# A two-block transformer step: where the W1 parts are stored, and which queue loads W2

## The reference, cut to what matters

```python
def film(x, cond, w, b):
    scale, shift = jnp.split(cond @ w + b, 2, axis=-1)
    return x * (1.0 + scale[:, None, :]) + shift[:, None, :]
h = film(rmsnorm(x, norm1_w), cond, film1_w, film1_b)
Q, K, V = h @ q_w + q_b, h @ k_w + k_b, h @ v_w + v_b
attn = softmax(Q @ K^T * D ** -0.5)                  # D = 512, one head
x = x + (attn @ V) @ proj_w + proj_b
h = film(rmsnorm(x, norm2_w), cond, film2_w, film2_b)
x = x + gelu(h @ mlp_w1 + mlp_b1) @ mlp_w2 + mlp_b2  # 512 -> 2048 -> 512
```

## Time and profile before

| | |
|---|---|
| time, median of 3 runs (lowest, highest) | 1500.64 us (1499.85, 1500.69) |
| the profiled execution: its own time | 1496.73 us |
| its span in the trace | 1494.9 us |
| TensorE busy | 1472.9 us (99% of the span) |
| VectorE, ScalarE, GpSimd busy | 940.5 us (63%), 669.4 us (45%), 625.4 us (42%) |
| W1 stores | 8 of 1792 KB, median 7.4 us from issue to landing |

### The profile page before, as it was taken

One profiled execution on the slowest core, in us unless ns is written; L12 is line 12 of the kernel. 1 busy time (PEld: TensorE's weight loads), 2 busy tenths in 40 slices (PEclk: granted clock), 3 DMA queues, 4 the chain that ended last, 5 costly groups with the idle time before them and its releaser, 6 DMA issues. The chain is left out here.

```text
span 1494.9 us, 24228 instructions
## 1 busy us (share of the span) xinstructions
PE 1472.9 (99%) x8712; PEld 1196.9 (80%) x8712; DVE 940.5 (63%) x1878; ACT 669.4 (45%) x2023; POOL 625.4 (42%) x544
## 2 busy tenths in 40 slices
PE   8999999999999999998999999999999999999999
PEld 5888888888888668777888778888888888888887
DVE  6677777777776677777767653764357434764354
ACT  4656555565644455555766433432224223432210
POOL 6756667676654447665856112301114102401001
PEclk9999999999999999999999999999999999999999
DMA  7222232222215435687554765535553554545342
GB/s 256 68 90 81 79 99 72 103 76 79 78 57 165 175 120 162 235 283 257 192 183 142 269 228 185 177 136 199 201 183 117 214 190 169 176 155 200 146 133 93
DMA packets 92919, 232.57 MB, mean 156 GB/s; under 512 B 9792, under 2 KB 17984, under 8 KB 87680
## 3 DMA queue, kind: packets, MB, share of 16 engines
q1 hardware_dynamic: 92128, 230.92, 44.6%
q10 hardware_dynamic: 672, 0.10, 0.0%
HBM read 174.17 MB, written 56.82 MB: 155 GB/s over the span
## 5 line engine op out<-in xcount | busy, mean ns | idle before, releaser
L1326 ACT ACTIVATE pa<-bank,neg_max 128x128 f32<-128x128 f32 x512 | 181.2, 408 | 136.5 <-DVE neg_max L1720 136.5
L724 PE MATMUL bank<-w_hi,g_hi 128*128 128x512 f32 x512 | 200.5, 392 | 0.0
L726 PE MATMUL bank<-w_hi,g_lo 128*128 128x512 f32 x512 | 199.3, 389 | 0.0
L725 PE MATMUL bank<-w_lo,g_hi 128*128 128x512 f32 x512 | 199.3, 389 | 0.0
L1218 PE MATMUL bank<-op_hi,ring 128*128 128x512 f32 x448 | 175.0, 391 | 2.5 <-DVE u2p L2140 1.4
L1222 PE MATMUL bank<-op_hi,ring 128*128 128x512 f32 x448 | 174.3, 389 | 0.0
L1220 PE MATMUL bank<-op_lo,ring 128*128 128x512 f32 x448 | 174.3, 389 | 0.0
L2278 POOL TENSOR_TENSOR xrc<-xrc,b 128x512 f32<-128x512 f32 x32 | 50.1, 1598 | 275.2 <-DMA xrc<-x_dram 275.2
L2306 POOL TENSOR_TENSOR pa<-pa,rec 128x512 f32<-128x512 f32 x128 | 142.8, 1125 | 51.9 <-DVE rec L1743 51.8
L1573 ACT ACTIVATE sum<-sum,cols 128x512 f32<-128x512 f32 x128 | 92.0, 722 | 112.6 <-DVE sum L2140 112.6
L1326 ACT ACTIVATION_READ_ACCUMULATOR pa<-bank,neg_max 128x1 f32 x512 | 126.9, 248 | 0.0
(11 more groups left out here) (263 smaller groups left out, 3553.6 us busy)
## 6 DMA issues: line engine op xcount, KB each, us to landing
ring<-w_dram SPq DMA_DIRECT2D x32, 1792.0 KB, 7.6
rows<-st_dram SPq DMA_DIRECT2D x32, 512.0 KB, 4.7
hid_dram<-sum SPq DMA_DIRECT2D x64, 256.0 KB, 2.2
hid<-hid_dram SPq DMA_DIRECT2D x64, 256.0 KB, 2.7
w_dram<-w_parts SPq DMA_DIRECT2D x8, 1792.0 KB, 7.4
xa<-xt_in SPq DMA_DIRECT2D x32, 256.0 KB, 4.2
xra<-xt_in SPq DMA_DIRECT2D x32, 256.0 KB, 2.8
x_dram<-h SPq DMA_DIRECT2D x32, 256.0 KB, 2.0
```

Source lines behind the costliest of these rows:

```text
L724: nc.tensor.matmul(dst, w_hi, a_hi, start=start, stop=False)
L725: nc.tensor.matmul(dst, w_hi, a_lo, start=False, stop=False)
L726: return nc.tensor.matmul(dst, w_lo, a_hi, start=False, stop=stop)
L1326: last = nc.scalar.activation(pa[:, j, m, :], scores_bank[j][:, m * P:(m + 1) * P], ACT.Exp, bias=neg_max[:, j * C + m:j * C + m + 1], acc ...
```

## The change

Its parts, in the order of the diff:

- `w2_pieces`: the pieces of W2 are split at one per half round: round 1 has 1 and 2, round 2 has 3 and 4, and so on.
- `t_first` has four slots in place of two. GpSimd makes the four samples' `t_first` (`rest_first`) one after the other, ahead of the last residual's bias; VectorE's low halves `low_first` move behind the softmax of sample 3.
- SyncE stores a group's first W1 piece where both stood (behind the third residual store). The second piece is stored one group later, behind the reload of residual 3. ScalarE splits the second piece behind the squares of samples 2 and 3, no longer ahead of them. VectorE's place for it stays.
- VectorE's `mean_square` of samples 0 and 1 moves from the start of the next group to the end of this one.
- The first round of stage C runs its products in the order 4, 0, 1, 2, 3, 5, 6, with bank 4 for products 4 and 6; `copy_ptb` of the last sample moves ahead accordingly.
- W2's pieces 2 to 7 are loaded from ScalarE's queue, each behind the split of the piece before; each piece is one transfer of 512 KB. Pieces 0 and 1 stay in SyncE's queue.

```diff
-    return ((), (0,)) if p == 0 else ((1,), ()) if p == 1 else ((2 * p - 2,), (2 * p - 1,)) if p < 5 else ((), ())
+    return ((), (0,)) if p == 0 else ((2 * p - 1,), (2 * p,) if p < 4 else ()) if p < 5 else ((), ())
...
+        def up_order(n):
+            return (4, 0, 1, 2, 3, 5, 6) if n == 0 else range(7)
+        def up_bank(n, r):
+            return bank[4] if n == 0 and r == 3 else bank[(UP_BANKS, DOWN_BANKS)[n // NP % 2][r]]
...
             def load_w2(i):
-                wait(sp, w2_lo_made, i - 1)
-                for v in range(2):
-                    f = f_tile(2 * i + v)
-                    sp.dma_start(stage_w2[i % 2][:, v], w2[f * P:(f + 1) * P, :]).then_inc(w2_in[i % 2], 16)
+                sp.dma_start(stage_w2[i % 2][:], w2_rows[i]).then_inc(w2_in[i % 2], 16)
...
                 load_bxr(g, GB - 1)
+                for i in w1_pieces(g - 1)[1:] if not first else ():
+                    store_w1(i)
...
                 store_x2(g, 2)
-                for i in w1_pieces(g):
+                for i in w1_pieces(g)[:1]:
                     store_w1(i)
...
-                    if first and p < 4:
-                        for i in ((2,), (3,), (4, 5), (6, 7))[p]:
-                            load_w2(i)
...
+                if n == 0:
+                    if i == 4:
+                        pe.wait_ge(op_lo_made, GB)
+                        pe.wait_ge(nb_free_act, GB * NG + 1)
+                        pe.wait_ge(ring_in[0], RING_IN + 16)
...
# ScalarE
-                for i in w1_pieces(g):
+                for i in w1_pieces(g)[:1]:
                     split_w1(i)
                 squares_b(g + 1, 2)
                 squares_b(g + 1, 3)
+                for i in w1_pieces(g)[1:]:
+                    split_w1(i)
...
                 nc.scalar.activation(w2_hi[:, 2 * i:2 * i + 2, :], stage_w2[i % 2][:], ACT.Identity)\
                     .then_inc(w2_hi_made, 1)
+                if 1 <= i < NP - 1:
+                    act.wait_ge(w2_lo_made, i)
+                    nc.scalar.dma_start(stage_w2[(i + 1) % 2][:], w2_rows[i + 1]).then_inc(w2_in[(i + 1) % 2], 16)
...
# VectorE
-                    if m == 0 and not first:
-                        mean_square(g + 1, 0, bssq, bxn, bvar)
-                        mean_square(g + 1, 1, bssq, bxn, bvar)
...
+                if not last:
+                    mean_square(g + 2, 0, bssq, bxn, bvar)
+                    mean_square(g + 2, 1, bssq, bxn, bvar)
+                if last:
+                    low_first(2)
+                    low_first(3)
...
# GpSimd
-                    if last:
-                        rest_first(b - 2)
...
+                    if last and b == GB - 1:
+                        for i in range(GB):
+                            rest_first(i)
```

More of the change, by code:

```diff
@@ L1182, in up_product @@
                 w, a, r, opens = PRODUCTS[i]
-                dst = bank[banks(s)[0][r]]
-                if s == 0 and p == 0:
-                    if i == 0:
+                dst = up_bank(n, r)
+                if n == 0:
[3 more added lines that the diff above has]
+                        pe.wait_ge(ring_in[0], RING_IN + 16)
+                    elif i == 0:
                         pe.wait_ge(blo, NB + GB)
@@ L1207, in up_product @@
                     pe.wait_ge(up_summed, 5 * n)
-                if i == 0:
+                    if n == 1:
+                        pe.wait_ge(x2_ready, NB)
+                if i == 0 and n > 0:
                     pe.wait_ge(ring_in[p % 2], RING_IN + 16 * (n // 2 + 1))
@@ L1211, in up_product @@
                     pe.wait_ge(up_copied, 2 * n + 1)
-                elif i == 5:
+                if i == 5:
                     pe.wait_ge(up_summed, 5 * n + 2)
@@ L1235, in down @@
                     wait(pe, y_ready, 8 * s)
+                    pe.wait_ge(up_summed, 5 * (NP * s + 1))
                 if half == 1 and k == 0:
@@ L1249, in body_c @@
                 for p in range(NP):
-                    for i in range(7):
+                    for i in up_order(NP * s + p):
                         up_product(s, p, i)
-                        if first and p == 0 and i == 0:
+                        if first and p == 0 and i == 4:
                             transpose_pb(NG - 1, GB - 1)
@@ L1562, in copy_up @@
             def copy_up(n, i):
[L1564 removed]
+                act.wait_ge(up_done, 7 * n + (1, 3)[i] + (n == 0))
                 if n > 0:
                     act.wait_ge(up_summed, 5 * n - (4, 0)[i])
[L1567 removed]
+                nc.scalar.activation((p1, u2)[i][:], up_bank(n, 0)[:], ACT.Identity).then_inc(up_copied, 1)
             def gelu(n, dst, count, half):
@@ L2023, in low_first @@
                 dve.wait_ge(op_hi_made, GB + b + 1)
-                low_half(op_lo[:, T1:N4 + 1, :, own], t_first[:, b % 2], op_hi[:, T1:N4 + 1, :, own])\
+                low_half(op_lo[:, T1:N4 + 1, :, own], t_first[:, b], op_hi[:, T1:N4 + 1, :, own])\
                     .then_inc(op_lo_made, 1)
@@ L2073, in body_b @@
                         norm_low_b(g + 1, b)
+                    if last and b == GB - 1:
+                        low_first(1)
                     low_v(g, b)
@@ L2077, in body_b @@
                         residual_b(g, b - 2)
-                    if b < GB - 1:
+                    if b < GB - 1 or last:
                         copy_ptb(g, b)
@@ L2087, in body_b @@
                         low_late(b - 1)
-                    if last and 0 < b < GB - 1:
-                        low_first(b - 1)
+                    if last and b == 1:
+                        low_first(0)
                 if g == 3:
@@ L2128, in add_up @@
                 up, copied, summed = ((2, 1, 0), (4, 2, 0), (5, 0, 2), (6, 2, 0), (7, 2, 0))[i]
-                r = banks(n // NP)[0][(1, 2, 3, 2, 3)[i]]
+                src_bank = up_bank(n, (1, 2, 3, 2, 3)[i])
                 dst, src = ((sum11, p1), (u2p5, u2), (sum22, u2p5), (sum12, u2), (sum21, u2))[i]
-                dve.wait_ge(up_done, 7 * n + up)
+                dve.wait_ge(up_done, 7 * n + up + (n == 0 and i < 2))
                 if copied:
@@ L2139, in add_up @@
                     wait(dve, hid_out[0], HID_OUT + 16 * n)
-                nc.vector.tensor_tensor(dst[:], bank[r][:], src[:], ALU.add).then_inc(up_summed, 1)
+                nc.vector.tensor_tensor(dst[:], src_bank[:], src[:], ALU.add).then_inc(up_summed, 1)
             def split_g(s, half, k, src):
@@ L2176, in body_c @@
             def body_c(s, first, last):
-                if first:
-                    copy_ptb(NG - 1, GB - 1)
-                    low_first(GB - 2)
-                    low_first(GB - 1)
-                else:
+                if not first:
                     for b in range(GB):
@@ L2372, in rest_first @@
                 own = slice(b * P, (b + 1) * P)
-                t1, t2, n4 = (t_first[:, b % 2, v] for v in range(3))
+                t1, t2, n4 = (t_first[:, b, v] for v in range(3))
                 pool.wait_ge(nb_free_act, GB * (NG - 1) + b + 3)
-                wait(pool, op_lo_made, GB + b - 1)
+                pool.wait_ge(rq_made, NB - GB)
                 then(combine(t1, h_late[:, 0:2, own], hb_new[:, 0:2, own]))
@@ L2411, in body_b @@
                     norm_late()
-                if last:
-                    rest_first(2)
-                    rest_first(3)
             each_group(body_b)
```

11 lines of the change are left out of this document (4 added, 7 removed).

## The result

The change makes the kernel slower by more than twice what was forecast: 1521.3 us median of 4 runs (1520.18 to 1523.6) against 1500.24 us (1497.42 to 1500.69), ratio 1.0144 (95% 1.0131 to 1.0157). The profiled execution took 1521.56 us, its span is 1519.8 us, 24.9 above the 1494.9 of before. That is 3.8 us more than the medians are apart: the execution profiled before was 3.5 us faster than the median of its kernel, the one profiled now 0.3 slower. The forecast was 1509.8 us, range 1500 to 1514.

What follows compares the result with a forecast made beforehand. TensorE was taken to bound the kernel, rarely resting, with ScalarE and VectorE just ahead of it. Terms 1.1 + 8.4 + 3.3 - 1.0 - 0.9 - 1.7 = +9.2 us on 1500.64 gave 1509.8 us, range 1500 to 1514.

Steps and rivals of the forecast that it cites:

- +8.4: Groups 2 and 3 as a pair: TensorE's transposes wait for the late second W1 store, +8.4 us, bounds 2.8 and 11.
- Group 1, +1.1: Group 1: ScalarE's second split, now behind the squares, delays `next_h` and TensorE's transpose by 1.1 us, bounds 0 and 1.9.
- Its landing, the split behind it and VectorE's half stay: First W1 piece in groups 2 and 3: store perhaps 0.2 us later, landing and wait for `tb` unchanged, nothing counted.
- Groups 2 and 3, +4.0 and +4.4: Second W1 piece: its late store, landing in 6.8 us, delays TensorE's transpose 4.0 us in group 2, 4.4 in group 3.
- The clock, +3.3: Groups 2 and 3: one new fall of the granted clock behind each longer wait, 1.6 and 1.7 us; bounds 0 and 3.3.
- Group 4, -1.0: Group 4: the store waited for goes alone, 6.8 us not 7.8; wait 3.31 becomes 2.3, clock still falls; bounds -5, 0.
- Start of stage C, -0.9: First round of stage C: new order gains 1.9 us, product 5's uncovered wait for `u2p` costs about 1.0; bounds -2.6, +1.
- W2, -1.7: Stage C: W2 loads from ScalarE's queue come early enough to remove waits for `u2p`, -1.7 us, bounds -1.7 and 0.
- Each piece is asked for at least half a round ahead: W2 in stage C: pieces requested this early should remove the `u2p` waits, part of the -1.7 us.
- what it takes away is the place behind a ring load: W2 in stage C: ScalarE's queue brings no bandwidth but frees loads from standing behind a ring load, part of -1.7 us.
- landings out of order: Rival: last residual store in groups 2 and 3 lands without waiting for earlier stores; sum +0.3, 1500.9 us; chance 0.19.
- the stores lengthen one another: Rival: paired W1 stores share engines, so each alone lands 1 us sooner; sum -8.3, 1492.3 us; chance 0.12.

Runs made afterwards that it cites:

- the split back: Changed kernel with ScalarE's second W1 split ahead of the squares again, the second store still late: 1518.36 us, ratio 1.0122 against the kernel before.
- The fillers: Changed kernel with short matmuls into unused columns, read by nobody, where TensorE waits in groups 2 to 4: 1513.35 us, ratio 1.0095 against the kernel before.
- a third slot: `w1_parts` given a third slot, so ScalarE's split waits for the store of three pieces earlier: kernel before 1505.25 us, changed kernel 1496.52 us.
- both edits together: Kernel before with the third W1 buffer and the late second store, ScalarE's split left early: 1485.62 us, ratio 0.9908.

## Why the prediction was wrong

For the W1 edits the direction, the chain and every place on it were right; the sizes were not. Their terms were +1.1, +8.4, +3.3 and -1.0, together +11.8 us, and the two edits alone cost 17.0. The step that failed is the landing of a store: 5.9 us for a first store and 6.8 for one alone were read from stores with other neighbours and at other places, where 7.0 to 8.7 us were measured. For stage C the sum had -2.6 us and all but the W1 edits cost +1.6 to +3.0: there the step that failed is W2's, by its sign. By its own steps:

- **Group 1, +1.1: measured +2.2.** The prediction gave the bounds 0 and 1.9 and took the cover of 0.88 us off the split. The cover was there (TensorE now follows the exp closely), but the squares themselves came 1.0 us later (605.25 in place of 604.26), as their tokens landed 5.0 us after issue in place of 4.0, and that used it up. With the split back 1.8 of it are gone.
- **"Its landing, the split behind it and VectorE's half stay": failed.** The first store of group 1 lands in 7.0 us, not in 5.9. The wait for `tb` behind it is 3.08 us, not 1.85, and everything that follows starts from there.
- **Groups 2 and 3, +4.0 and +4.4: +6.0 and +6.6 before the clock.** In group 2 the second store was to be issued at 636.9, or 638.0 with group 1's 1.1. It was issued at 640.62: 1.2 because the first store was later than that, 1.3 because the reload came 11.56 us behind the first store and not 10.3, which is the slower landing again (the reload is 4.6 us behind that landing; the prediction had 4.3). Then it landed in 7.2 us in place of 6.8, in group 3 in 8.7. From landing to transpose the sum had 0.15 + 1.88 + 3.09 = 5.1 us; measured 5.2. Of the 2.0 us that group 2 is over its term, 1.4 are these two landings and 0.3 is the reload behind the first. The bound of 7.8 was too low as well, for group 3's.
- **The clock, +3.3: about +5.3 for the two new falls.** The waits were 6.5 and 6.0 us, not 4 and 6, and the falls behind them cost 2.6 and 2.7 us where those of before cost 1.6 and 1.7. The fillers show that they are paid to the idle time.
- **Group 4, -1.0: +2.0, the wrong sign.** The store of piece 4 goes alone, and takes 8.1 us, no less than as the first of two (7.8). The wait is 4.17 us in place of 3.31, and the stretches at 720 and 730 us lose 1.6 + 1.8 us in place of 1.7. The 6.8 us of the earlier trace rows belong to piece 6's store at the end of the next group, and the 7.8 to piece 4's own place, where it hardly changes with what stands behind it. So the -1.0 took a price of the place for a price of the neighbour.
- **Start of stage C, -0.9: -1.35, given back.** The wait for `pb` of 1.12 us is gone, and the new wait of product 5 behind it is 0.78 us, where the sum had about 1.0. The new round alone measures -0.7 us with an interval from -2.1 to +0.6, which holds the -0.9 and holds nothing as well. What stage C gives back belongs mostly to the next term.
- **W2, -1.7: about +2, the wrong sign.** "Each piece is asked for at least half a round ahead" holds, and half a round is not enough: the third piece took 10.0 us. The prediction said that no row shows such a load and then gave it no bound above nothing. What failed is "what it takes away is the place behind a ring load": behind a ring load W2's landing is as long from ScalarE's queue as from SyncE's (7.2 to 10.0 us now, 7.2 to 10.6 before). By the Trainium skill (DMA: Bandwidth & Descriptors, "Issuing engines are not separate DMA queues") DMAs of all issuers interleave on the same engines; the trace agrees, since ScalarE's loads took 7.2 to 10.0 us when a ring load of SyncE was ahead of them or started with them, and 4.0 to 4.4 us otherwise.

Of the rivals, "landings out of order" and "the stores lengthen one another" fell with the first landing of 7.0 us. The second had the right question, whether a store's time depends on what goes beside it, and the wrong sign: the other W1 store behind it is a gentler neighbour than the token and residual loads. Of stage C's +3.95 W2 is about 2; the kernels with the new round and W2 as before show +1.0 to +3.65 in the same stretch, from one execution each, so the division of the rest is open. What no part of the prediction saw is that the squares already waited for their tokens in groups 2 and 3; it reads ScalarE as going from the split straight to them. That did not enter the sum, but it is why the same store's place turns from a loss into a gain with a third slot.

## What to carry to other kernels

Before moving a transfer to a later place in its queue, ask who waits for its landing and how many buffers lie between: here the same move costs 12 to 15 us with two slots and gains some 20 with three (1505.25 to 1485.62). A wait that is taken away uncovers the next one in the same queue, so a third buffer alone made this kernel slower (1.0039), and both edits together made it 0.9908. And a landing time that is read from one row of its kind is a bound, not a term: here one and the same transfer landed after 5.8 to 8.7 us when it went alone or first of a pair.

## What the runs showed of the hardware

- A store of 1792 KB, 128 rows of 14 KB, landed at the same two places in 5.9 us with another one issued right behind it, in 7.0 us with smaller loads behind it, and in 5.8 and 6.2 us with nothing behind it in its queue. At other places it took 7.0 to 8.7 us with loads behind it and 5.8 to 8.0 us with nothing.
- A 512 KB load from ScalarE's queue landed after 3.2 to 10.6 us in the nine kernels that have it there; in the changed one after 7.2 to 10.0 us when a 1792 KB load of SyncE was ahead of it or started with it, and after 4.0 to 4.4 us otherwise.
- The length of a wait did not decide by itself whether the granted clock fell: it fell behind one of 1.85 us before and not behind one of 3.08 us in the changed kernel. Behind the waits of 6.5 and 6.0 us 2.6 and 2.7 us were lost. With short matmuls in the same waits it stayed at 1.00 in all of them.
- Three kernels with the same program up to stage C had their clock falls at different groups: their transposes of group 5 stood 3.1, 4.5 and 4.1 us behind those of before in one execution each. A shift of a few microseconds between two traces is not by itself the price of an edit.
